# Two Perceiver layers in fp32: a latent attention layer as one block, and experts that gather their tokens by index

## What is computed

```python
logits = x @ wr                                  # 1024 tokens, 8 experts
top1, top2 = two best experts of each token
loc1 = cumsum(onehot(top1)) - 1                  # place of the token in its expert's list
loc2 = cumsum(onehot(top2)) - 1 + onehot(top1).sum(0)
buf[top1, s1] = x ; buf[top2, s2] = x            # C = 256 places an expert, later tokens are dropped
y = relu(buf @ w1 + b1) @ w2 + b2                # per expert, 256 -> 1024 -> 256
out = g1 * y[top1, s1] + g2 * y[top2, s2]
```

```python
c_q, c_kv = x @ W_DQ, x @ W_DKV                  # 256 -> 64
Qc, Qr = c_q @ W_UQ, rope(c_q @ W_QR)            # 16 and 8 channels a head
Kc, V  = c_kv @ W_UK, c_kv @ W_UV
Kr     = rope(x @ W_KR)                          # one for all heads
w = softmax(causal(clip(Qc Kc + Qr Kr, -80, 80)) / sqrt(24))
x = x + (w @ V) @ W_O
```

## Time and profile before

| | |
|---|---|
| median of three runs | 994.61 us (992.96 to 995.33) |
| the profiled execution's own time | 992.36 us |
| its span | 990.6 us |
| busy in the span | TensorE 841.5 us (85%), VectorE 589.6 (60%), ScalarE 430.1 (43%), GpSimd 339.4 (34%) |
| mean granted TensorE clock | 0.90 of full speed |
| expert block, from VectorE's first norm to its last row | 521.9 to 679.4 us |
| latent block and its attention | 819.65 to 898.1 us |
| last block | 898.4 to 990.6 us |

### The profile page before, as it was taken

The page is one execution under the profiler, slowest core; times in us unless marked ns, Lnnn a source line. Parts: engine busy times, 40 slices in busy tenths (PEclk is TensorE's granted clock), DMA queues, the critical chain, the costliest instruction groups (busy, mean ns, idle before and its releaser), DMA issues. The chain is left out here.

```text
span 990.6 us, 19998 instructions
## 1 busy us (share of the span) xinstructions
PE 841.5 (85%) x7396; PEld 631.3 (64%) x7396; DVE 589.6 (60%) x1374; ACT 430.1 (43%) x1245; POOL 339.4 (34%) x466
## 2 busy tenths in 40 slices
PE   5999997975999999759685399994789996687998
PEld 4888885434999999635464288883567773464344
DVE  3555556376999999671857032233696775463751
ACT  3666564657644550135444000000476663663730
POOL 2112111046999999210332800003533331250000
PEclk9999999887999999768795599997599997798999
DMA  7113500000000000000200255534353200000001
GB/s 237 31 33 102 187 13 2 1 0 1 1 1 2 1 1 1 1 1 0 87 2 28 85 159 172 189 107 143 110 153 90 73 24 0 2 3 1 1 1 43
DMA packets 45284, 51.72 MB, mean 52 GB/s; under 512 B 7205, under 2 KB 40850, under 8 KB 45060
## 3 DMA queue, kind: packets, MB, share of 16 engines
q1 hardware_dynamic: 40644, 43.47, 13.9%
q0 software_dynamic: 1536, 4.08, 1.3%
q10 hardware_dynamic: 3008, 2.88, 0.8%
HBM read 43.20 MB, written 7.34 MB: 51 GB/s over the span
## 5 line engine op out<-in xcount | busy, mean ns | idle before, releaser
L656 POOL TENSOR_TENSOR r_faded<-r_state,rec_f 128x256 f32<-128x256 f32 x128 | 82.1, 642 | 17.5 <-DVE r_state L635 7.2
L683 PE MATMUL r_u_ps<-r_t_in,l_same_head 128*128 128x256 f32 x256 | 87.1, 422 | 0.2
L662 POOL TENSOR_TENSOR r_q_in<-r_state,rec_q 128x256 f32<-128x256 f32 x128 | 82.1, 641 | 0.3 <-DVE r_state L635 0.2
L690 PEld LDWEIGHTS r_o_ps<-l_head_of,r_q_in 128*128 128x128 f32 x512 | 77.3, 192 | 6.9 <-POOL r_q_in L662 0.4
L1360 ACT ACTIVATE a_prob<-a_s_ps,a_negmax 128x256 f32<-128x256 f32 x128 | 59.0, 488 | 41.2 <-DVE a_negmax L1397 41.2
L1020 ACT ACTIVATE a_prob<-a_s_ps,a_negmax 128x256 f32<-128x256 f32 x128 | 59.1, 486 | 19.7 <-DVE a_negmax L1076 19.7
L690 PE MATMUL r_o_ps<-l_head_of,r_q_in 128*128 128x8 f32 x512 | 65.4, 236 | 0.3 <-POOL r_q_in L662 0.3
L628 DVE TENSOR_TENSOR r_update<-r_u_ps,rec_k 128x256 f32<-128x256 f32 x128 | 55.2, 431 | 6.8 <-PE r_u_ps L683 6.8
L1896 PE MATMUL m_h_ps<-m_rowsT,l_w 128*128 128x256 f32 x256 | 58.2, 387 | 0.3 <-ACT m_rowsT L1939 0.3
L1818 DVE TENSOR_SCALAR m_hidden<-m_h_ps,l_b 128x256 f32<-128x256 f32 x64 | 28.0, 479 | 48.7 <-PE m_h_ps L1896 48.7
L635 DVE TENSOR_TENSOR r_state<-r_update,r_faded 128x256 f32<-128x256 f32 x128 | 54.3, 424 | 4.4
(11 more groups left out here) (321 smaller groups left out, 1983.2 us busy)
## 6 DMA issues: line engine op xcount, KB each, us to landing
l_w<-in_B_w SPq DMA_DIRECT2D x16, 1024.0 KB, 6.0
a_ctxT<-in_ctxT SPq DMA_DIRECT2D x31, 256.0 KB, 2.8
a_ctx<-in_ctx SPq DMA_DIRECT2D x16, 256.0 KB, 3.2
expert_rows<-ffn_zeros SPq DMA_DIRECT2D x8, 256.0 KB, 2.9
m_rows<-expert_rows SPq DMA_DIRECT2D x8, 256.0 KB, 5.9
expert_out<-m_y ACTq DMA_DIRECT2D x7, 256.0 KB, 6.5
all_X<-in_x SPq DMA_DIRECT2D x4, 256.0 KB, 5.4
l_b<-in_B_b SPq DMA_DIRECT2D x1, 1024.0 KB
```

What stands on the lines that cost most here:

```text
L656: nc.gpsimd.tensor_tensor(faded[m][:, :, :], state[(t + 1) % 2][m][:, :, :], row("f", t, m), ALU.mult).then_inc(faded_ready[m], 1)
L662: nc.gpsimd.tensor_tensor(q_in[t % 2][m][:, :, :], state[t % 2][m][:, :, :], row("q", t, m), ALU.mult).then_inc(q_ready[m], 1)
L683: nc.tensor.matmul(u_ps[t % 2][m][:, 0:B, :], same_head[:, :], t_in[m][:, :, :], start=False, stop=True).then_inc(u_mm[m], 1)
L690: mm = nc.tensor.matmul(o_ps[:, 2 * m + c, :, t % U], q_in[t % 2][m][:, c * (B // 2):(c + 1) * (B // 2), :], head_of[:, :], start=True, st ...
```

## The change

There are two parts.

**Experts gather.** `xn`, the normalised rows, is stored by SyncE to `routed_rows` in device memory (eight DMAs of 128 rows, behind each scaled tile). Instead of the row where a token goes, the block works out which token each of the 2048 rows holds: for each token and choice VectorE makes a one-hot row of its place within 128 (`row_hot`) and one of its expert and half (`part_hot`), the latter times its partition and times its tile's number (`hot_rows`, L1755 of the new kernel); 16 small bf16 matmuls (`tokens`, L1883) add them up in PSUM; VectorE sums the two parts and converts (`token`). GpSimd fetches the rows of an expert with two indirect DMAs (`gather_rows`, L1843): those of experts 0 and 1 first, then `b2` and X, then the other six experts. Scatters, zeroing and SyncE's `load_rows` are gone. The norms stand together at the front of VectorE's queue, and ScalarE takes its four square roots sooner. A table `route` (128x153) is loaded at the start.

**One latent block.** `latent_attention_stage` holds the inputs and the attention. The inputs of the second half are put between the first steps of attention; four PSUM banks go round for everything except the scores; turned rows go two tiles to a bank. `batch_attention_stage` is left for the third step alone.

```diff
-                def rows_of(ts, c):
-
-                    step.link(nc.vector.scalar_tensor_tensor(row[:, ts, c], chosen[:, ts, c], float(CAP), place[:, ts, c], ALU.mult, ALU.add))
+                def hot_rows(ts, c):
+
+                    n = ts.stop - ts.start
+                    nc.vector.tensor_scalar(upper[:, ts, c], place[:, ts, c], P + 0.5, float(P), ALU.is_gt, ALU.mult)
                     step.link(nc.vector.tensor_scalar(over[:, ts, c], place[:, ts, c], CAP + 0.5, 2.0 * ROWS, ALU.is_gt, ALU.mult))
-                    nc.vector.scalar_tensor_tensor(slot_kept[:, ts, c], row[:, ts, c], -1.0, over[:, ts, c], ALU.add, ALU.add).then_inc(kept_ready, 1)
+                    nc.vector.tensor_tensor(row[:, ts, c], place[:, ts, c], upper[:, ts, c], ALU.subtract)
+                    step.link(nc.vector.scalar_tensor_tensor(part_at[:, ts, c], chosen[:, ts, c], float(CAP), upper[:, ts, c], ALU.mult, ALU.add))
+                    nc.vector.tensor_tensor(over[:, ts, c], over[:, ts, c], part_at[:, ts, c], ALU.add)
+                    step.link(nc.vector.tensor_tensor(row_hot[:, ts, c, :], row[:, ts, c].unsqueeze(2).to_broadcast([P, n, P]), row_no.unsqueeze(1).to_broadcast([P, n, P]), ALU.is_equal))
+                    step.link(nc.vector.tensor_tensor(part_hot[:, ts, c, :], over[:, ts, c].unsqueeze(2).to_broadcast([P, n, PARTS]), part_no.unsqueeze(1).to_broadcast([P, n, PARTS]), ALU.is_equal))
+                    nc.vector.tensor_scalar(token_hot[:, ts, c, 0, :], part_hot[:, ts, c, :], place_no, None, ALU.mult)
+                    nc.vector.tensor_tensor(token_hot[:, ts, c, 1, :], part_hot[:, ts, c, :], tile_no[:, ts].unsqueeze(2).to_broadcast([P, n, PARTS]), ALU.mult).then_inc(hot_ready, 1)
...
-                    if g >= 2:
-                        choices(g - 2)
-                    if g >= 3:
-                        first_places(g - 3)
-                choices(3)
-                first_places(2)
-                first_places(3)
+                choices(0)
+                for g in range(1, NT // 2):
+                    choices(g)
+                    first_places(g - 1)
+                first_places(NT // 2 - 1)
...
-                rows_of(every, 1)
+                hot_rows(every, 1)
...
+                dve.wait_ge(token_mm, ONE + 1)
+                step.link(nc.vector.tensor_reduce(token_sum[:, :], token_ps.rearrange("p i h -> p h i"), AX.X, ALU.add))
+                nc.vector.tensor_copy(token[:, :], token_sum[:, :]).then_inc(token_ready, 1)
...
-                pool.wait_ge(*cleared)
-                for t in range(NT):
-                    pool.wait_ge(kept_ready, ONE + t // 2 + 1)
-                    scatter(t, 0)
-                pool.wait_ge(kept_ready, ONE + NT // 2 + 1)
-                for t in range(NT):
-                    scatter(t, 1)
+                def gather_rows(e):
+                    if e >= 2:
+                        pool.wait_ge(xt_mm, ONE + e - 1)
+                    for c in range(2):
+                        nc.gpsimd.indirect_dma_start(out=rows[e % 2][:, c, :], out_offset=None, in_=xn_d, in_offset=bass.IndirectOffsetOnAxis(ap=token[:, 2 * e + c:2 * e + c + 1], axis=0)).then_inc(rows_in[e % 2], 16)
+
+                pool.wait_ge(stored, ONE + 16 * NT)
+                pool.wait_ge(token_ready, ONE + 1)
+                gather_rows(0)
+                gather_rows(1)
                 nc.gpsimd.tensor_scalar(b2[:, :, :], b2[:, :, :], 1.0 - DROPOUT, None, ALU.mult).then_inc(b2_ready, 1)
                 for t in range(NT):
                     nc.gpsimd.tensor_tensor(X[:, t, :], X[:, t, :], Y[:, t, :], ALU.add).then_inc(x_summed, 1)
+                for e in range(2, E):
+                    gather_rows(e)
...
-                sp.wait_ge(scattered, 16 * 2 * NT)
-                load_rows(0)
-                load_rows(1)
-                load_rows(2)
+                for t in range(NT):
+                    sp.wait_ge(normed.scaled, ONE + t + 1)
+                    sp.dma_start(xn_d[t * P:(t + 1) * P, :], xn[:, t, :]).then_inc(stored, 16)
```

The queues of the latent block in the new kernel (TensorE, then the middle of ScalarE's, then VectorE's):

```diff
+                first_products(0)
+                plain_channels(0)
+                others(0)
+                scores(0)
+                first_products(1)
+                scores(1)
+                transposes(0)
+                plain_channels(1)
+                heads(0)
+                others(1)
+                transposes(1)
+                output(0)
+                scores(2)
+                heads(1)
+                scores(3)
+                for u in (2, 3):
+                    transposes(u)
+                    output(u - 1)
+                    heads(u)
+                output(NU - 1)
...
+                for i in range(2):
+                    take_values(0, i)
+                for r in range(4):
+                    exps(0, r)
+                take_turned(2)
+                take_turned(3)
+                take_low(1)
+                for n in range(4):
+                    take_transposed(0, n)
+                for r in range(4):
+                    exps(1, r)
...
+                for u in (2, 3):
+                    for r in range(4):
+                        shift(u, r)
+                    denominators(u)
+                    add(u - 1)
+                add(NU - 1)
```

More of the change, by code:

```diff
@@ L1875, in totals, with tokens @@
                     mm.then_inc(count_mm, 1)
+                def tokens(ts, c):
+                    pe.wait_ge(hot_ready, ONE + (ts.stop // 2 if c == 0 else NT // 2 + 1))
+                    for t in range(ts.start, ts.stop):
+                        mm = nc.tensor.matmul(token_ps, row_hot[:, t, c, :], token_hot[:, t, c, :, :], start=(c == 0 and t == 0), stop=(c == 1 and t == NT - 1))
+                    if c == 1:
+                        mm.then_inc(token_mm, 1)
                 def turn_rows(e):
                     j = e % 2
-                    pe.wait_ge(rows_in[j], ONE + 16 * (e // 2 + 1))
+                    pe.wait_ge(rows_in[j], 32 * (e // 2 + 1))
                     if e >= 2:
@@ L1919, in _ @@
                 totals()
+                for g in range(NT // 2):
+                    tokens(slice(2 * g, 2 * g + 2), 0)
+                tokens(slice(0, NT), 1)
                 turn_rows(0)
@@ L1988, in _ @@
                     if e + 2 < E:
-                        load_rows(e + 2)
                         load_first(e + 2)
@@ new lines, in plain, with rest, turning, headed @@
+        def plain(c):
+            return [use for m in range(KD) for use in ((("q", c, m), (q_ready, ONE + KD * c + m + 1)), (("k", c, m), (k_ready, ONE + KD * c + m + 1)))]
+        def rest(c):
+            return [use for i in range(2) for use in ((("qr", c, i), (qr_taken, ONE + 2 * c + i + 1)), (("v", c, i), (v_ready, ONE + 2 * c + i + 1)))]
+        def turning(u):
+            return [(("t", u, n), (pt_ready, ONE + 4 * u + n + 1)) for n in range(4)]
+        def headed(u):
+            return [(("o", u), (heads_ready, ONE + u + 1))]
@@ L2027, in bank, with added, of_bank @@
+        def added(u):
+            return [(("out", u), (x_added, ONE + u + 1))]
+        uses = latents(0) + plain(0) + rest(0) + latents(1) + turning(0) + plain(1) + headed(0) + rest(1) + turning(1) + added(0) + headed(1)
+        for u in (2, 3):
+            uses += turning(u) + added(u - 1) + headed(u)
+        uses += added(NU - 1)
+        place = {what: n for n, (what, _) in enumerate(uses)}
         def bank(*what):
             return banks[place[what] % RING]
+        def of_bank(u, r):
+            return prob[u % 2][:, 4 * r:4 * r + 4, :, :].rearrange("p q e s -> p (q e) s")
@@ L2030, in over_positions, with where @@
+        def where(q):
+            return q // 2 % 2, 4 * (q % 2) + q // 4
         def over_positions(table):
@@ new lines, in output @@
+                def output(u):
+                    pe.wait_ge(heads_ready, ONE + u + 1)
+                    acc = free_bank("out", u)
+                    for i in range(2):
+                        for k in range(KD):
+                            mm = nc.tensor.matmul(acc[:, i * D:(i + 1) * D], headsT[:, i, k, :], Wo[:, k, :], start=(k == 0), stop=(k == KD - 1))
+                    mm.then_inc(out_mm, 1)
+                first_products(0)
+                plain_channels(0)
+                others(0)
@@ L2124, in _, with rotated @@
+                for u in (2, 3):
+                    for n in range(4):
+                        take_transposed(u, n)
+                        if u + 1 < NU:
+                            exps(u + 1, n)
+                    take_heads(u)
             @block.vector
             def _(dve):
-                def turned(c, i, name, mm, taken, out):
+                def rotated(c, i, name, mm, taken, out):
                     dve.wait_ge(mm, ONE + 2 * c + i + 1)
@@ new lines, in _ @@
+                for i in range(2):
+                    rotated(1, i, "kr", kr_mm, kr_taken, turned_k)
+                for r in range(4):
+                    shift(1, r)
```

(11 more changed lines are left out.)

295 lines of the change are left out of this document (194 added, 101 removed).

## The result

The changed kernel takes **990.89 us** (median of 13 runs, 989.79 to 992.48) against 994.61 us for the kernel before in 13 runs beside it. The ratio is **0.9965**, 95% interval 0.995 to 0.9979: 3.5 us faster (2.1 to 5.0), which is more than 0.2%. The profiled execution took 991.28 us with a span of 989.5, TensorE's mean granted clock 0.90.

What follows compares the result with a forecast made beforehand. TensorE's 20.11 us wait for scattered rows bounds the expert block, a chain through all five engines the latent block; -8.4 + 7.0 = -1.4 us from the 994.6 median gives 993.2 us, range 988.8 to 998.0.

Steps and rivals of the forecast that it cites:

- Part 1: Expert block, gathers instead of scatters: first layer 8.9 us earlier, +0.5 for low clock, together -8.4 us.
- Part 2: One latent block: +2.3 us of layout at full clock and +4.7 of low clock, together +7.0 us, between +2.3 and +10.
- first pause: Latent block, after scores 0: TensorE waits 3.3 us (845.7 to 849.0) for ScalarE's copies of the second half's turned rows.
- second pause: Latent block, after output 1: TensorE waits 4.6 us (885.1 to 889.7) for values 2.
- I take 4.7, above the middle, as the nearest row for the long pause did fall: Latent block: price of the clock dropping in TensorE's two pauses, +4.7 us, chosen between 0 and 7.7.
- at full clock all along: Latent block: the last shift waits behind `add(1)`, so the block ends at 900.4 instead of 898.1, +2.3 us.
- The +10 us: Latent block: size of part 2 if, by the skill's rule, both TensorE pauses cost in full.
- Rival 3: Latent block: both pauses start cold and slower, next block too (+1); +11 us, time 997.2; chance 0.2.
- Rival 1: Latent block: the clock stays up; part 2 is +2.3 to +3.5, time 989.1; chance 0.2.
- Rival 2: Latent block: the overlap pays, second half hides beside attention, 5.05 us pause gone; -5 us, time 981; chance 0.08.
- So nothing is gained: Latent block: the 5.05 us pause goes, but 5.4 us of second-half products and others move into the middle.
- Rival 4: Expert block: gathers come late, indices 2.9 later or landing 5.7; part 1 is -5.6, time 996.2; chance 0.1.

Runs made afterwards that it cites:

- experiment 1: The changed kernel with the latent stages of before, so only the experts' part is changed: 985.32 us, ratio 0.991 to the kernel before.
- experiment 8: The kernel before with only the norms together at the front and the square roots sooner, scatters kept: 987.28 us, ratio 0.9962.
- experiment 4: The changed kernel with the second half's rows turned ahead of scores 0 and copied ahead of step 0's exponentials: 984.46 us, ratio 0.9903.
- experiment 7: The changed kernel with three extra TensorE products in the pause between scores 0 and the second half's products: 985.68 us, ratio 0.9942.
- experiment 3: The changed kernel with the additions of output 1 and 2 moved behind the last step's sums on VectorE: 983.32 us, ratio 0.9903.
- experiment 2: The kernel before with the one latent block, so only the latent part is changed: 999.87 us, ratio 1.0055.
- experiments 5: The changed kernel with both latent moves, additions behind the last sums and second half turned and copied earlier: 972.71 us, ratio 0.9816.

## Why the prediction was right and wrong

The time was forecast as 993.2 us with a range of 988.8 to 998.0 and no measurable change as its likeliest case; it is 990.89, measurably faster and inside the range. The sum was -1.4 us and should have been -3.5.

**Part 1 was right.** Forecast -8.4, measured -8.9 in the medians (experiment 1, 7.3 to 10.6) and -7.9 in the pair of profiles. Step by step from the block's first norm, in us:

| step | forecast | after |
|---|---|---|
| choices begin | 6.3 | 6.3 |
| tail begins | 20.6 | 20.7 |
| indices ready | 24.5 | 25.0 |
| first gather | 25.3 | 25.9 |
| fourth gather to its landing | 2.9 | 2.8 |
| first layer | 33.0 | 33.6 |
| one-hot of 1024 numbers | 1.2 | 1.22 |
| extra low clock in the first layer | +0.5 | +0.67 |

The tail was 0.6 us longer than forecast, and 0.5 of it passes through every later step. Nothing behind the four gathers came late: the next one starts at 562.92, as `b2` and X end. What the prediction didn't say is that part of the gain has nothing to do with gathers (experiment 8).

**Part 2 had the right mechanism, with its clock priced too high and its layout too slow.** From the latent block's first norm:

| step | forecast | after |
|---|---|---|
| scores 0 start | 22.5 | 21.9 |
| first pause, length | 3.3 | 3.3 |
| first pause ends | 29.4 | 28.2 |
| scores 1 end | 37.4 | 37.1 |
| scores 2 start | 52.4 | 53.0 |
| division 2 | 59.0 | 59.0 |
| output 1 ends | 65.5 | 65.5 |
| last shift | 66.2 | 66.2 |
| second pause, length | 4.6 | 4.6 |
| last division | 69.9 | 70.0 |
| last addition ends | 80.8 | 81.9 |

The rows agree within 0.7 us except at the end of the first pause and at the end of the block, but in part by luck, as two errors cancel on the way. The layout gave a step of scores 2.67 us, from a row of before (870.93 to 873.60) in which TensorE has gaps of its own; at full clock it takes 2.0 (836.88 to 838.89). And it had the first pause end 1.1 us late. The low clock, which the layout leaves out, filled that room.

What it cost on the chain can be estimated from rows: 1.49 us on the latent product; 0.7 us between the last transposes of step 1 and scores 2 (4.86 us from 863.18 to 868.04, and 4.18 in experiment 4 at full clock); and 0.9 us from the last division's start to the last addition's end (11.88, before 10.96). In the second pause, values 2 took 1.93 instead of 1.10 and transposes 3 took 3.68, but the last division covers them until 889.1.

The step that failed is "I take 4.7, above the middle, as the nearest row for the long pause did fall": 4.7 of low clock against about 3.1 by these rows. The +2.3 "at full clock all along" was too much as well: of the 3.4 us that the block is longer in the profiles, some 0.3 are left for it. In the medians part 2 is +5.5, where the forecast had +7.0. The profile before isn't a firm base either: both first steps of scores ran at the low clock in it (0.50 in 855 to 865), while in experiment 1, with the same stages, the second step began at full clock (0.67 in 855.9 to 860.9), and that block is 3.0 us shorter.

The rule of the Trainium skill ("TensorE: Matmul & The Clock Gate", section "HAM oscillation — how this bites in real kernels") that each short run of matmuls behind such a wait starts cold agrees for both pauses (3.47 us for 1.98 behind the one, 1.93 for 1.10 behind the other). The +10 us drawn from it didn't come, since the key products had full clock already and the slow ones of the second pause lay beside the division. Behind a shorter wait of 2.29 us scores 0 went either way, at full clock in the changed kernel (2.0 us) and low in experiment 7 (3.3 us).

**Rivals.** Rival 3 (slower by both pauses) had the clock's fall right and its price wrong, and the last block didn't begin slower (+0.1 us, forecast +1). Rival 1 (989.1) had the time nearly right and the reason wrong, since the clock didn't stay up. Rival 2's argument against itself, `add(1)` ahead of the last shift, is what experiment 3 confirms: without it the new block is level with the old (75.24 against 75.80 in the same session). "So nothing is gained" about the overlap was too strong: with both waits out of the way the same overlap brings the block to 68.8 us, 7 to 10 under the old one. Rival 4 didn't happen (its own terms give 996.0, not 996.2).

**What no step had** is the spread of blocks that the change doesn't touch. It was +4.0 in the profiled pair and would have read as a failure of part 1 or 2 if only totals had been compared.

## What to carry to other kernels

When work is moved into the gaps of another stage, read each in-order queue at the seam for an instruction that needn't be there: here an addition ahead of the last shifts and two copies behind four exponentials cost 12 to 15 us together, more than the overlap had to give. Price a low clock only for the work that lies on the chain, and look for the engine that covers the rest. An edit that brings TensorE back earlier out of a long wait may only move work into the slow stretch. And compare block by block, with the same kernel's profile taken twice, before a difference of a few micros in one block is explained. A layout by hand that agrees row by row can still hold two errors; compare the lengths of its pieces too.

## What the runs showed of the hardware

- The same kernel on two chips had the block over the context at 129.56 and at 133.33 us, from when TensorE's clock rose: 24 us after the block's start in the one and more than 37 in the other. The Trainium skill ("TensorE: Matmul & The Clock Gate", section "Part 1: The HAM clock gate") says that the number of slow matmuls of one kernel differs between runs; these profiles agree.
- The clock's rise didn't follow the start of the first layer: 1.2 us earlier work, and the clock at 0.50 until 558 and 0.61 or 0.63 in 558 to 560 either way.
- The low clock behind one and the same wait costs differently from profile to profile: behind the first pause of 3.2 to 3.3 us it was 1.5 us in the changed kernel (3.47 and 3.60 us for the two products) and 3.1 in experiment 2 (3.78 and 4.88).
- VectorE's scaling of two tiles takes 0.70 us, but 2.12 at the start of the latent block, beside a memset of GpSimd; in the changed kernel, VectorE, then GpSimd:

```profile
816.85 2.12 DVE L142 TENSOR_SCALAR a_rows<-all_X,a_x_meanvar,a_x_rstd 128x256 f32<-128x256 f32 x2
...
819.76 0.70 DVE L142 TENSOR_SCALAR a_rows<-all_X,a_x_meanvar,a_x_rstd 128x256 f32<-128x256 f32 x2
```

```profile
814.99 3.51 POOL L2386 MEMSET mla_vals<- 128x4096 f32 x1 [4.22 <-POOLq L1200]
```

That the memset causes it wasn't tried; experiments 5 and 8 have the same 2.12 at that place.
